# A state-space layer: B by transposes of one product, raw steps left in PSUM, and the next group's jobs dealt out anew

## The chip, the cores and the metric

The program runs on one core of a Trainium2 chip. The metric is device time in microseconds (us) of one execution, the median of several. Five engines work side by side, each through its own queue in order: TensorE (PE, products), VectorE (DVE), ScalarE (ACT), GpSimd (POOL) and SyncE (SP, which issues transfers). They meet only at semaphores.

## The reference

Six layers follow each other over 64 sequences of 128 steps and 128 features, each behind a residual sum and a normalisation. The change touches only the first, a selective state-space layer (the other five are left out here):

```python
def _ssm_forward(u, W_in, b_in, W_x, b_x, W_dt, b_dt, A_log, D, W_out, b_out):
    u_inner = u @ W_in.T + b_in
    x, z = jnp.split(u_inner, 2, axis=-1)              # 256 channels each
    dbc = x @ W_x.T + b_x
    delta_raw = dbc[..., :DT_RANK]                     # 8
    B_ssm = dbc[..., DT_RANK:DT_RANK + D_STATE]        # 16
    C_ssm = dbc[..., DT_RANK + D_STATE:]               # 16
    delta = jax.nn.softplus(delta_raw @ W_dt.T + b_dt)
    A = -jnp.exp(A_log)

    def step(h, xs):
        dt_t, x_t, Bt, Ct = xs
        dA = jnp.exp(dt_t[..., None] * A)
        dB = dt_t[..., None] * Bt[:, None, :]
        h = h * dA + x_t[..., None] * dB
        y_t = jnp.einsum('bdn,bn->bd', h, Ct)
        return (h, y_t)
    ...
    y = y + x * D
    y = y * (z * jax.nn.sigmoid(z))
    return y @ W_out.T + b_out

x = _layernorm(x + _L0_attn_ref(x, ...), axis=-1)
```

## The kernel before

`ssm_phase` works on 16 groups of four sequences (`GT` = 512 columns). A group is eight units, which I call steps 0 to 7: step p takes four of the 16 states (nq = p // 2) of one half of the 256 channels (half = p % 2). All arithmetic is fp32. In each step the engines do this:

- TensorE writes x·delta·B of the unit to the PSUM tile `db`: 16 small products (L349) of `dxT` with `diag`, a block-diagonal form of B. `db` has one buffer, so they wait for the scan of the step before (`h_ready`).
- ScalarE writes the decays `dA` of the next step: four Exp (L438).
- VectorE scans 2048 elements (L494), h = h·dA + db, and multiplies one state in four by C (L500, here hC on VectorE).
- GpSimd multiplies the other three by C (L556). Both factors lie in SBUF, on both engines.
- TensorE adds up y of two steps earlier: four products with the identity (L363). In the first unit of each half, x·D comes ahead of them as the product L358 ("the skip").

Beside these steps of group g, `head(g + 1, ..., p)` makes the inputs of the next group, a piece behind each step, and the code with `there(g - 1)` finishes the group before. Both stand in each engine's queue in the order of `step`, between two steps, and an engine that waits in one holds up the next step. The pieces of the next group:

- step 0: x (L306), read by ScalarE into `xi`. Step 1: w_x times x (L309, L310) gives C (rows 0 to 15) and the raw step (rows 32 to 39), read by ScalarE into `dbc` (L400). B is made apart, turned already: eight products with x as the stationary side (L314), to which VectorE adds the bias (L476, tile `Bt`).
- step 2: w_dt times the raw step (L322); ScalarE adds the bias and stores `dtr` (L407). Step 3: |dtr|, Exp, Ln (L410 to L414) into `spl`. Step 4: VectorE's `delta` = max(dtr, 0) + spl, 1024 elements (L481).
- steps 3 and 4: GpSimd makes `diag` (L536, four in all). Step 5: z (L328, Silu on ScalarE, L420) and, on GpSimd, dx = delta·x (L544). Step 6: eight transposes of dx (L334), copied to `dxT`.

Of the group before: VectorE's gate `yg` in steps 1 and 2 (L507); in step 4 the output product (L372) and, on VectorE, the residual sum r (L514) and its statistics (L117, L121); in step 3 GpSimd's `xr` = X + bias (L562), in step 5 its inverse deviation and shift (L126, L128, L571, L574); in step 6 ScalarE's normalised result (L452).

The PSUM is full: `db` has four banks, y two, `pj[0]` and `pj[1]` one each. All products for the next group and the output product share the last two.

## Time and profile before

| | us |
|---|---|
| median of 3 runs | 4159.24 |
| lowest and highest | 4155.75, 4160.47 |
| the profiled execution | 4173.35 |
| its span in the trace | 4171.5 |
| first scan of the layer starts | 33.56 |
| last scan of the layer starts | 981.67 |
| groups 1 to 14, mean each | 60.64 |

The layer takes the first 1004 us of the span; the other five phases, whose code is the same in both kernels, take the rest. A group is eight scans, so the start of one scan to the start of the next is the yardstick: the eight distances of a group add up to the group. The last row of the table is 848.90 us by 14. The page gives TensorE 83% busy over the span, VectorE 60%, GpSimd 48%, ScalarE 47%.

### The profile page before, as it was taken

Reading aid. Unit: us, or ns where it says so; the run is one execution under the profiler, and the core shown is the slowest. Engines: PE = TensorE matmul, PEld = TensorE weight load, DVE = VectorE, ACT = ScalarE, POOL = GpSimd, SP = SyncE. Lnnn points to the kernel's source line nnn. Section 1 sums busy time; section 2 is a strip of 40 time slices with the busy share of each in tenths; the row PEclk is TensorE's granted clock in tenths of the full one; section 3 lists DMA queues with packets and bytes.
Section 4 is the critical chain, followed back from the end, with each engine's and each line's share of the span. In section 5 each row is a group of like instructions: output and inputs, shape, how many; then the busy total and the mean of one; then the engine's idle time right before and its main releaser. Section 6 shows DMA issues by size and latency. Waiting matters only on the chain. (4 is left out here: it accounts for less than half of the span.)

```text
span 4171.5 us, 104540 instructions
## 1 busy us (share of the span) xinstructions
PE 3456.3 (83%) x41696; PEld 2257.9 (54%) x41696; DVE 2515.9 (60%) x5780; ACT 1949.0 (47%) x3810; POOL 2008.4 (48%) x1742
## 2 busy tenths in 40 slices
PE   7898889886888888777999979778888688888576
PEld 3444444443455555554666657645555455556476
DVE  6877877785656565474555548656666543433265
ACT  5555555552444444333555544245555344443154
POOL 5666766664567676561111116346666300102455
PEclk8999999997999999897999989879999788885598
DMA  3211212114600000000000000000000000000286
GB/s 117 77 74 76 76 68 77 70 74 156 218 2 2 2 2 2 15 15 4 5 5 5 4 10 1 10 1 0 0 0 0 10 5 6 5 4 14 76 260 194
DMA packets 48939, 181.24 MB, mean 43 GB/s; under 512 B 11678, under 2 KB 23073, under 8 KB 39360
## 3 DMA queue, kind: packets, MB, share of 16 engines
q1 hardware_dynamic: 44224, 167.68, 12.0%
q0 software_dynamic: 4352, 8.47, 0.6%
q8 instruction: 259, 4.24, 0.4%
q14 instruction: 104, 0.85, 0.1%
HBM read 167.13 MB, written 43.65 MB: 51 GB/s over the span
## 5 line engine op out<-in xcount | busy, mean ns | idle before, releaser
L494 DVE TENSOR_TENSOR_SCAN XC<-ssm_dA,ssm_db 128x2048 f32<-128x2048 f32 x128 | 565.6, 4419 | 148.3 <-PE ssm_db L349 124.7
L556 POOL TENSOR_TENSOR XC<-XC,XB 128x1536 f32<-128x1536 f32 x128 | 493.5, 3856 | 297.9 <-DVE XC L494 165.9
L363 PE MATMUL ssm_y<-XC,ssm_wt 128*128 128x512 f32 x1024 | 495.5, 629 | 1.6 <-POOL XC L556 1.6
L438 ACT ACTIVATE ssm_dA<-ssm_delta,ssm_nega 128x508 f32<-128x508 f32 x512 | 325.0, 707 | 107.3 <-DVE XC L494 107.3
L1138 POOL TENSOR_TENSOR self_pm<-self_pT,self_wt 128x512 f32<-128x512 f32 x256 | 320.9, 1291 | 68.7 <-ACT self_pT L912 68.7
L363 PEld LDWEIGHTS ssm_y<-XC,ssm_wt 128*128 128x128 f32 x1024 | 197.0, 200 | 230.8 <-issue 221.5
L2326 POOL TENSOR_TENSOR XC<-XC,gla_wt 128x512 f32<-128x512 f32 x128 | 160.7, 1276 | 159.5 <-ACT XC L2177 159.5
L1149 POOL TENSOR_TENSOR XC<-XC,XB 128x128 f32<-128x128 f32 x128 | 58.9, 460 | 363.9 <-DVE XB L1055 363.9
L349 PE MATMUL ssm_db<-XB,ssm_dxT 32*128 32x128 f32 x4096 | 175.4, 300 | 69.5 <-DVE XC L494 67.8
L126 POOL TENSOR_SCALAR narrow_rstd<-narrow_mv 128x4 f32<-128x4 f32 x16 | 3.6, 228 | 458.6 <-DVE narrow_mv L121 458.6
L349 PEld LDWEIGHTS ssm_db<-XB,ssm_dxT 32*128 32x128 f32 x4096 | 146.3, 199 | 135.0 <-DVE XC L494 110.9
L912 ACT ACTIVATE self_pT<-self_scores 128x512 f32<-128x512 f32 x256 | 132.2, 603 | 179.9 <-PE self_scores L799 179.9
L1404 ACT ACTIVATE narrow_pT<-narrow_scores 77x512 f32<-77x512 f32 x256 | 130.7, 592 | 132.4 <-PE narrow_scores L1337 132.4
L912 ACT ACTIVATE cross_pT<-cross_scores 77x512 f32<-77x512 f32 x256 | 130.8, 590 | 122.9 <-PE cross_scores L799 122.9
L2336 POOL TENSOR_TENSOR XC<-XC,gla_wt 128x512 f32<-128x512 f32 x128 | 160.9, 1278 | 35.0 <-ACT XC L2186 34.5
L1044 DVE TENSOR_TENSOR self_oT<-self_out,self_rinv 128x512 f32<-128x512 f32 x64 | 44.3, 692 | 207.2 <-ACT self_rinv L940 207.2
L1600 PEld LDWEIGHTS mlp_yp<-mlp_wt,mlp_h 128*128 128x128 f32 x1024 | 133.2, 192 | 58.1 <-issue 56.4
L1033 DVE TENSOR_REDUCE self_nmax<-self_scores 128x4 f32<-128x512 f32 x256 | 158.7, 683 | 9.2 <-PE self_scores L787 8.9
L1455 DVE TENSOR_TENSOR narrow_oT<-narrow_out,narrow_rinv 128x128 f32<-128x128 f32 x64 | 18.7, 292 | 239.1 <-ACT narrow_rinv L1413 173.3
L1044 DVE TENSOR_TENSOR cross_oT<-cross_out,cross_rinv 128x512 f32<-128x512 f32 x64 | 44.1, 688 | 186.7 <-ACT cross_rinv L940 178.5
L2259 DVE TENSOR_TENSOR XC<-gla_scores,gla_wt 128x512 f32<-128x512 f32 x128 | 82.4, 685 | 102.1 <-PE gla_scores L2051 102.1
L1628 ACT ACTIVATE mlp_h<-mlp_hp,mlp_bias 128x512 f32<-128x512 f32 x128 | 87.9, 687 | 108.6 <-PE mlp_hp L1592 108.4
(431 smaller groups left out, 8934.0 us busy)
## 6 DMA issues: line engine op xcount, KB each, us to landing
XB<-c_rows SPq DMA_DIRECT2D x64, 1024.0 KB, 4.5
experts_we<-in_w_experts SPq DMA_DIRECT2D x72, 579.0 KB
sorted<-in_padding SPq DMA_DIRECT2D x1, 33280.0 KB
experts_rt<-sorted SPq DMA_DIRECT2D x72, 65.0 KB
ssm_xT<-in_xT SPq DMA_DIRECT2D x16, 256.0 KB, 4.6
self_wt<-in_w_self SPq DMA_DIRECT2D x1, 1412.0 KB, 6.1
...
```

Source lines behind the costliest of these rows:

```text
L349: mm = pe.matmul(of_batch(db, b)[:, :, 32 * c:32 * c + 32], dxT[rows, slot, half, c, :], diag(slot, c)[rows, nq, :].rearrange("p (k t) -> ...
L363: mm = pe.matmul(yp[half][:, :].rearrange("p (b t) -> p b t", b=GROUP), ident, of_state(states(32, at), k), start=False, stop=(nq == 3 and ...
L438: o = act.activation(dA[:, p % 2, :].rearrange("p (b k t) -> p b k t", b=GROUP, k=4)[:, :, k, 1:T], by_batch(delta[:, slot, half, :])[:, : ...
L494: dve.tensor_tensor_scan(states(0, p).rearrange("p m t -> p (m t)"), dA[:, p % 2, :], db[:, :], 0.0, ALU.mult, ALU.add).then_inc(h_ready, 1)
L556: pool.tensor_tensor(states(32, p).rearrange("p (b k) t -> p b k t", k=4)[:, :, 0:3, :], states(0, p).rearrange("p (b k) t -> p b k t", k= ...
L912: act.activation(pT[0:TK, b % 2, r, :], sc[r][0:TK, :], ACT.Exp).then_inc(exp_ready, 1)
L1033: dve.tensor_reduce(nmax[:, r, :], sc[r][:, 0:4 * TK].rearrange("p (h t) -> p h t", h=4), AX.X, ALU.max, negate=True).then_inc(max_ready, 1)
L1138: pool.tensor_tensor(pm[:, b % 2, r, :].rearrange("p (h t) -> p h t", h=4), pT[:, b % 2, r, :].rearrange("p (h t) -> p h t", h=4), bcast(V ...
L1404: act.activation(pT[0:TK, b % 2, r, :], sc[r][0:TK, :], ACT.Exp).then_inc(exp_ready, 1)
L1600: mm = pe.matmul(yp[g % 2][:, b * C:(b + 1) * C], h[:, g % 2, j, b * T:(b + 1) * T], w3[:, j * C:(j + 1) * C], start=(j == 0), stop=(j == 3))
L2326: pool.tensor_tensor(a1(b, r), a1(b, r), bcast(tri, 1, 4), ALU.mult).then_inc(m1_pool, 1)
L2336: pool.tensor_tensor(a2(b, r), a2(b, r), bcast(tri0, 1, 4), ALU.mult).then_inc(m2_pool, 1)
```

## The change

B. w_x gets 80 rows: C in 0 to 15, the raw step in 32 to 39, B in 64 to 79, and a row 40 of zeros whose bias is 1.0. ScalarE reads rows 0 to 40 as before (batches reordered) and rows 64 to 79 in a second instruction, with their biases. Four transposes of those 16 rows, in step 2, replace the eight products of step 1, and ScalarE copies the result to `Bt` in VectorE's place.

Raw steps. Row 40 of `dbc` is a row of ones, and w_dt gets b_dt as its ninth row, so the product carries its bias. `dtr` is gone: |raw| is read from PSUM by two ScalarE instructions of 512 in step 2, and VectorE's `delta`, now in step 3, reads the raw steps from PSUM too (`pair`, the two banks as one tile). Until then both banks are held: the output product waits for `dt_ready`, and so does z, whose first half now goes to `pj[1]` and the second to `pj[0]`.

Jobs. The sum r moves from step 4 to 5, its statistics to 6; GpSimd's `xr` from 3 to 2, its inverse deviation from 5 to 6; the normalised result from 6 to 7. The skip of half 0 moves from the half's first unit (step 2) to its third (step 6). The second half of z, into `pj[0]`, waits for r (`r_ready`), which has been read from that bank.

```diff
-    PJ, N_ACT, DT, YS = 10, 9, 4, 2
+    PJ, N_ACT, DT, YS = 10, 9, 5, 2
...
+    SKIP = ((0, 2), (1, 0))
...
+        STEP = slice(32, 41)
+        INPUT = slice(64, 80)
...
-        pj = [ph.bank(f"pj{i}") for i in range(2)]
+        pair = ph.stack.enter_context(nc.psum_tensor(f"{name}_pj", [P, 2, GT], F32))
+        pj = [pair[:, i, :] for i in range(2)]
...
+                if p == 2:
+                    pe.wait_ge(proj_read, at + 4)
+                    pe.sem_inc(mark, 1)
                     for c in range(4):
-                        for j in range(2):
-                            mm = pe.matmul(pj[1][:, c * N:(c + 1) * N], xi[:, slot, j, c * P:(c + 1) * P],
-                                           w_xB[:, j * N:(j + 1) * N], start=(j == 0), stop=(j == 1))
+                        mm = pe.transpose(pj[1][:, c * N:(c + 1) * N], dbc[INPUT, c * P:(c + 1) * P], ident[INPUT, INPUT])
                     mm.then_inc(proj_mm, 1)
-                if p == 2:
-                    pe.wait_ge(proj_read, at + 3)
                     for j in range(2):
                         if j == 1:
-                            pe.wait_ge(Bt_ready, g + 1)
-                        pe.matmul(pj[j][:, :], w_dt[32:32 + 8, j * P:(j + 1) * P], dbc[32:32 + 8, :]).then_inc(proj_mm, 1)
+                            pe.wait_ge(proj_read, at + 5)
+                        pe.matmul(pj[j][:, :], w_dt[STEP, j * P:(j + 1) * P], dbc[STEP, :]).then_inc(proj_mm, 1)
                 if p == 5:
+                    pe.wait_ge(dt_ready, (g + 1) * DT)
                     for j in range(2):
-                        pe.wait_ge(proj_read, at + 4 + j)
-                        if j == 0 and needed(g - 1):
+                        if j == 1 and needed(g - 1):
                             pe.wait_ge(r_ready, g - 1)
-                        pe.matmul(pj[j][:, :], w_in[:, (2 + j) * P:(3 + j) * P], xT[:, slot, :]).then_inc(proj_mm, 1)
+                        pe.matmul(pj[1 - j][:, :], w_in[:, (2 + j) * P:(3 + j) * P], xT[:, slot, :]).then_inc(proj_mm, 1)
...
-                        if nq == 0:
-                            if needed(gy * YS):
-                                pe.wait_ge(y_step, (gy - 1) * YS + half + 1)
+                        if nq == 0 and needed(gy * YS):
+                            pe.wait_ge(y_step, (gy - 1) * YS + half + 1)
+                        if (half, nq) in SKIP:
                             pe.matmul(chunked(yp[half][:, :]), skip[:, half, :],
-                                      by_chunk(xi[:, slot if p >= 2 else 1 - slot, half, :]), start=True, stop=False)
+                                      by_chunk(xi[:, slot if p >= 2 else 1 - slot, half, :]), start=(nq == 0), stop=False)
...
                         if more(g) and there(g):
-                            pe.wait_ge(proj_read, (g + 1) * N_ACT + 4)
+                            pe.wait_ge(dt_ready, (g + 2) * DT)
...
                 if p == 2:
+                    act.wait_ge(proj_mm, at + 4)
...
+                    act.activation(Bt[:, :], pj[1][:, 0:GROUP * N], ACT.Identity).then_inc(proj_read, 1)
                     for j in range(2):
                         act.wait_ge(proj_mm, at + 5 + j)
...
-                        act.activation(dtr[:, j, :], pj[j][:, :], ACT.Identity, bias=b_dt[:, j:j + 1]).then_inc(proj_read, 1)
+                        act.activation(spl[:, j, :], pj[j][:, :], ACT.Abs).then_inc(dt_ready, 1)
                 if p == 3:
-                    act.wait_ge(proj_read, g * N_ACT + 5)
-                    act.activation(spl[:, :, :], dtr[:, :, :], ACT.Abs).then_inc(dt_ready, 1)
...
-                if p == 4:
-                    dve.wait_ge(dt_ready, g * DT + 3)
+                if p == 3:
+                    dve.wait_ge(dt_ready, g * DT + 4)
...
                     dve.scalar_tensor_tensor(delta[:, slot].rearrange("p a t -> p (a t)"),
-                                             dtr[:, :, :].rearrange("p a t -> p (a t)"), 0.0,
+                                             pair[:, :, :].rearrange("p a t -> p (a t)"), 0.0,
                                              spl[:, :, :].rearrange("p a t -> p (a t)"), ALU.max, ALU.add)\
```

What this makes of the queues, at three places of a group in the loop. L349 and L350 are the products into `db`, L363 and L364 those of y (one line on in the kernel after).

TensorE from the end of step 1's pieces to the w_dt products of step 2; L314 and L318 make B, L322 and L323 the raw steps, L358 is the skip. Before:

```order
L314 MATMUL ssm_pj<-ssm_wt,ssm_xi 128x16 x8
L345 REGISTER_ALU
L349 MATMUL ssm_db<-XB,ssm_dxT 128x4x32 [waits ssm_h_ready]
L349 MATMUL ssm_db<-XB,ssm_dxT 128x4x32 x15
L357 ISA
L358 MATMUL ssm_y<-ssm_xi,ssm_skip 128x512 [waits ssm_y_step]
L363 MATMUL ssm_y<-XC,ssm_wt 128x512 [waits ssm_hC_pool,ssm_hC_dve]
L363 MATMUL ssm_y<-XC,ssm_wt 128x512 x3
L318 REGISTER_ALU
L322 MATMUL ssm_pj<-ssm_dbc,ssm_wt 128x512 [waits ssm_proj_read]
L321 REGISTER_ALU
L322 MATMUL ssm_pj<-ssm_dbc,ssm_wt 128x512 [waits ssm_Bt_ready]
```

After:

```order
L346 REGISTER_ALU
L350 MATMUL ssm_db<-XB,ssm_dxT 128x4x32 [waits ssm_h_ready]
L350 MATMUL ssm_db<-XB,ssm_dxT 128x4x32 x15
L357 ISA
L364 MATMUL ssm_y<-XC,ssm_wt 128x512 [waits ssm_hC_pool,ssm_hC_dve,ssm_y_step]
L364 MATMUL ssm_y<-XC,ssm_wt 128x512 x3
L315 REGISTER_ALU
L318 MATMUL ssm_pj<-ssm_wt,ssm_dbc 128x16 [waits ssm_proj_read]
L318 MATMUL ssm_pj<-ssm_wt,ssm_dbc 128x16 x3
L323 MATMUL ssm_pj<-ssm_dbc,ssm_wt 128x512
L322 REGISTER_ALU
L323 MATMUL ssm_pj<-ssm_dbc,ssm_wt 128x512 [waits ssm_proj_read]
```

The 16 passes of L314 stood between w_x and the next step's products; now nothing does, the skip is gone from this step, and four transposes stand ahead of w_dt.

VectorE from one scan (L494, printed as SCALAR_TENSOR_TENSOR) to the next, with delta (L481), r (L514) and the statistics. Before, steps 4 to 5:

```order
L494 SCALAR_TENSOR_TENSOR XC<-ssm_dA,ssm_db 128x2048 [waits ssm_hC_pool,ssm_dA_ready,ssm_dB_mm]
L199 REGISTER_ALU [waits ssm_h_ready]
L500 TENSOR_TENSOR XC<-XC,XB 128x4x128 [waits ssm_y_mm,ssm_c_in0]
L514 TENSOR_TENSOR ssm_r<-ssm_pj,ssm_xr 128x512 [waits ssm_x_out,ssm_xr_ready,ssm_out_mm]
L117 BN_STATS ssm_stats<-ssm_r 128x6 [waits ssm_r_ready]
L117 BN_STATS ssm_stats<-ssm_r 128x6 x3
L121 BN_AGGR ssm_mv<-ssm_stats 128x2 [waits ssm_vec]
L121 BN_AGGR ssm_mv<-ssm_stats 128x2 x3
L478 REGISTER_ALU
L481 SCALAR_TENSOR_TENSOR ssm_delta<-ssm_dtr,ssm_spl 128x1024 [waits ssm_dA_ready,ssm_dt_ready]
L490 REGISTER_ALU
L494 SCALAR_TENSOR_TENSOR XC<-ssm_dA,ssm_db 128x2048 [waits ssm_hC_pool,ssm_dA_ready,ssm_dB_mm]
```

After, steps 3 to 5:

```order
L494 SCALAR_TENSOR_TENSOR XC<-ssm_dA,ssm_db 128x2048 [waits ssm_hC_pool,ssm_dA_ready,ssm_dB_mm]
L500 TENSOR_TENSOR XC<-XC,XB 128x4x128 [waits ssm_y_mm,ssm_c_in1,ssm_h_ready]
L478 ISA
L481 SCALAR_TENSOR_TENSOR ssm_delta<-ssm_pj,ssm_spl 128x1024 [waits ssm_dA_ready,ssm_dt_ready]
L490 REGISTER_ALU
L494 SCALAR_TENSOR_TENSOR XC<-ssm_dA,ssm_db 128x2048 [waits ssm_hC_pool,ssm_dA_ready,ssm_dB_mm]
L201 REGISTER_ALU [waits ssm_h_ready]
L500 TENSOR_TENSOR XC<-XC,XB 128x4x128 [waits ssm_y_mm,ssm_c_in0]
L490 REGISTER_ALU
L494 SCALAR_TENSOR_TENSOR XC<-ssm_dA,ssm_db 128x2048 [waits ssm_hC_pool,ssm_dA_ready,ssm_dB_mm]
L500 TENSOR_TENSOR XC<-XC,XB 128x4x128 [waits ssm_y_mm,ssm_c_in0,ssm_h_ready]
L514 TENSOR_TENSOR ssm_r<-ssm_pj,ssm_xr 128x512 [waits ssm_x_out,ssm_xr_ready,ssm_out_mm]
```

One distance held r, statistics and delta; now delta has step 3, r step 5, and the statistics have gone to step 6.

GpSimd from step 5's multiplication by C (L556, after: L557) on; dx is L544, after: L545. Before:

```order
L556 TENSOR_TENSOR XC<-XC,XB 128x4x384 [waits ssm_y_mm,ssm_c_in0,ssm_h_ready]
L126 TENSOR_SCALAR ssm_rstd<-ssm_mv 128x4 [waits ssm_vec,ssm_x_out]
L127 REGISTER_ALU
L128 TENSOR_TENSOR ssm_rstd<-ssm_rstd,ssm_power 128x4 [waits ssm_pool_step]
L570 REGISTER_ALU
L571 TENSOR_TENSOR ssm_shift<-ssm_mv,ssm_rstd 128x4 [waits ssm_pool_step]
L572 REGISTER_ALU
L574 TENSOR_SCALAR ssm_shift<-ssm_shift 128x4 [waits ssm_pool_step]
L540 REGISTER_ALU
L542 REGISTER_ALU [waits ssm_dt_ready]
L544 TENSOR_TENSOR ssm_dx<-ssm_delta,ssm_xi 128x4x4x32 [waits ssm_proj_mm]
L544 TENSOR_TENSOR ssm_dx<-ssm_delta,ssm_xi 128x4x4x32
```

After:

```order
L557 TENSOR_TENSOR XC<-XC,XB 128x4x384 [waits ssm_y_mm,ssm_c_in0,ssm_h_ready]
L541 ISA
L543 REGISTER_ALU [waits ssm_dt_ready]
L545 TENSOR_TENSOR ssm_dx<-ssm_delta,ssm_xi 128x4x4x32 [waits ssm_proj_mm]
L545 TENSOR_TENSOR ssm_dx<-ssm_delta,ssm_xi 128x4x4x32
L553 REGISTER_ALU
L557 TENSOR_TENSOR XC<-XC,XB 128x4x384 [waits ssm_y_mm,ssm_c_in1,ssm_h_ready]
L126 TENSOR_SCALAR ssm_rstd<-ssm_mv 128x4 [waits ssm_vec,ssm_x_out]
L127 REGISTER_ALU
L128 TENSOR_TENSOR ssm_rstd<-ssm_rstd,ssm_power 128x4 [waits ssm_pool_step]
L571 REGISTER_ALU
L572 TENSOR_TENSOR ssm_shift<-ssm_mv,ssm_rstd 128x4 [waits ssm_pool_step]
```

The inverse deviation and shift stood between step 5 and dx; now they follow step 6's multiplication.

## Rows read from the trace of the kernel before

**Rows 1.** The page: its head.
```profile
span 4171.5 us, 104540 instructions
```
**Rows 2.** Busy time by stretch, groups 1 to 14: us, busy (count) of each engine, PEclk.
```profile
89.90:149.80 59.90, 54.37 (x381) 29.24 (x381) 48.22 (x29) 32.90 (x51) 41.77 (x20) 0.94 0.21 76
...
sum 848.90, PE 755.77 PEld 406.54 DVE 674.84 ACT 460.15 POOL 583.85; mean PE 53.98 PEld 29.04 DVE 48.20 ACT 32.87 POOL 41.70
```
**Rows 3.** VectorE in order of time, group 8: start, us, operation, [idle before <-releaser].
```profile
514.01 4.42 DVE L494 TENSOR_TENSOR_SCAN XC<-ssm_dA,ssm_db 128x2048 f32<-128x2048 f32 x1 [0.74 <-PE ssm_db L349]
...
520.38 4.42 DVE L494 TENSOR_TENSOR_SCAN XC<-ssm_dA,ssm_db 128x2048 f32<-128x2048 f32 x1 [1.06 <-PE ssm_db L349]
...
528.85 4.42 DVE L494 TENSOR_TENSOR_SCAN XC<-ssm_dA,ssm_db 128x2048 f32<-128x2048 f32 x1 [0.81 <-POOL XC L556]
...
536.14 4.42 DVE L494 TENSOR_TENSOR_SCAN XC<-ssm_dA,ssm_db 128x2048 f32<-128x2048 f32 x1 [1.44 <-PE ssm_db L349]
...
541.86 4.42 DVE L494 TENSOR_TENSOR_SCAN XC<-ssm_dA,ssm_db 128x2048 f32<-128x2048 f32 x1 [0.47 <-PE ssm_db L349]
...
549.30 3.42 DVE L481 SCALAR_TENSOR_TENSOR ssm_delta<-ssm_dtr,ssm_spl 128x1024 f32<-128x1024 f32 x1
552.64 4.41 DVE L494 TENSOR_TENSOR_SCAN XC<-ssm_dA,ssm_db 128x2048 f32<-128x2048 f32 x1
...
558.34 4.42 DVE L494 TENSOR_TENSOR_SCAN XC<-ssm_dA,ssm_db 128x2048 f32<-128x2048 f32 x1 [0.57 <-PE ssm_db L349]
...
570.21 4.42 DVE L494 TENSOR_TENSOR_SCAN XC<-ssm_dA,ssm_db 128x2048 f32<-128x2048 f32 x1 [6.72 <-PE ssm_db L349]
```
**Rows 4.** TensorE in order of time, group 8, same columns.
```profile
519.14 1.17 PE L349 MATMUL ssm_db<-XB,ssm_dxT 32*128 32x128 f32 x32
...
525.72 1.96 PE L314 MATMUL ssm_pj<-ssm_wt,ssm_xi 128*128 128x16 f32 x16
527.61 1.17 PE L349 MATMUL ssm_db<-XB,ssm_dxT 32*128 32x128 f32 x32
528.71 1.12 PE L358 MATMUL ssm_y<-ssm_xi,ssm_skip 128*128 128x512 f32 x2
529.67 3.60 PE L363 MATMUL ssm_y<-XC,ssm_wt 128*128 128x512 f32 x8
533.20 0.69 PE L322 MATMUL ssm_pj<-ssm_dbc,ssm_wt 8*128 8x512 f32 x1
...
545.26 1.95 PE L372 MATMUL ssm_pj<-ssm_wt,ssm_yg 128*128 128x128 f32 x16
547.13 1.17 PE L349 MATMUL ssm_db<-XB,ssm_dxT 32*128 32x128 f32 x32
...
551.77 1.88 PE L328 MATMUL ssm_pj<-ssm_xT,ssm_wt 128*128 128x512 f32 x4
```
**Rows 5.** TensorE in order of time, group 8, around its step 6.
```profile
566.15 1.96 PE L334 MATMUL ssm_pj<-ssm_wt,ssm_dx 128*128 128x128 f32 x8 [4.25 <-POOL ssm_dx L544]
568.05 2.09 PE L349 MATMUL ssm_db<-XB,ssm_dxT 32*128 32x128 f32 x32
```
**Rows 6.** VectorE by line, whole run: ns min/median/max, first and last start.
```profile
L481 DVE SCALAR_TENSOR_TENSOR ssm_delta<-ssm_dtr,ssm_spl x16: 1226/3426/4459, 20.2 to 914.2; 128x1024 f32<-128x1024 f32 x16
...
L500 DVE TENSOR_TENSOR XC<-XC,XB x128: 691/693/1604, 38.0 to 986.1; 128x512 f32<-128x512 f32 x128
...
L507 DVE TENSOR_TENSOR ssm_yg<-ssm_y,ssm_zs x32: 682/684/692, 101.3 to 994.0; 128x512 f32<-128x512 f32 x32
```
**Rows 7.** GpSimd in order of time, group 8, step 5.
```profile
561.15 0.23 POOL L126 TENSOR_SCALAR ssm_rstd<-ssm_mv 128x4 f32<-128x4 f32 x1
...
563.55 2.47 POOL L544 TENSOR_TENSOR ssm_dx<-ssm_delta,ssm_xi 128x512 f32<-128x512 f32 x2
```
**Rows 8.** ScalarE in order of time, group 8, step 3.
```profile
540.40 1.06 ACT L414 ACTIVATE ssm_spl<-ssm_spl 128x1024 f32<-128x1024 f32 x1
```
**Rows 9.** TensorE by stretch: us, busy (count), PEclk, DMA share, GB/s.
```profile
265.00:270.00 5.00, 5.00 (x30) 0.63 0.00 0
```

More of the change, by code:

```diff
@@ L164, in ssm_phase @@
         zs = ph.sb("zs", [P, 2, 2, GT])
-        dbc = ph.sb("dbc", [64, GT])
+        dbc = ph.sb("dbc", [80, GT])
         Bt = ph.sb("Bt", [P, GROUP * N])
-        dtr = ph.sb("dtr", [P, 2, GT])
         spl = ph.sb("spl", [P, 2, GT])
@@ L363, in step @@
                             mm = pe.matmul(yp[half][:, :].rearrange("p (b t) -> p b t", b=GROUP), ident,
-                                           of_state(states(32, at), k), start=False, stop=(nq == 3 and k == 3))
+                                           of_state(states(32, at), k), start=(k == 0 and nq == 0 and (half, 0) not in SKIP),
+                                           stop=(nq == 3 and k == 3))
                         mm.then_inc(y_mm, 1)
@@ L419, in head @@
                             act.wait_ge(y_step, (g - 1) * YS)
-                        act.activation(zs[:, slot, j, :], pj[j][:, :], ACT.Silu, bias=b_in[:, 2 + j:3 + j]).then_inc(proj_read, 1)
+                        act.activation(zs[:, slot, j, :], pj[1 - j][:, :], ACT.Silu, bias=b_in[:, 2 + j:3 + j]).then_inc(proj_read, 1)
                     act.preload_act_table_set("natural_log_exp_and_others")
@@ L448, in step @@
                             decay(g + 1, 1 - slot, 0)
-                    if p == 6 and there(g - 1):
+                    if p == 7 and there(g - 1):
                         act.wait_ge(pool_step, g * 4)
@@ L508, in step @@
                             .then_inc(y_step, 1)
-                    if p == 4 and there(g - 1):
+                    if p == 5 and there(g - 1):
                         dve.wait_ge(out_mm, g)
@@ L514, in step @@
                         dve.tensor_tensor(r[:, :, :], by_batch(pj[0][:, :]), xr[:, :, :], ALU.add).then_inc(r_ready, 1)
+                    if p == 6 and there(g - 1):
                         dve.wait_ge(r_ready, g)
@@ L531, in head @@
                 if p in (3, 4):
-                    pool.wait_ge(Bt_ready, g + 1)
+                    pool.wait_ge(proj_read, g * N_ACT + 5)
                     if needed((g - 1) * U):
```

45 lines of the change are left out of this document (20 added, 25 removed).

## The prediction

> **What bounds the kernel now.** I read the busy times first, then one group of the loop engine by engine in order of time, and at each scan asked what it had waited for. The layer in question is the first 1004 us of a span of 4171.5 [rows 1]; the rest is the same code. Groups 1 to 14 take 848.90 / 14 = 60.64 us each, and TensorE is busy for 53.98 of them [rows 2]. So no engine is full, but TensorE is near: what is taken off another engine's chain can shorten a group by about six us and little more, unless TensorE's own work shrinks or it is busy now at a lower clock.
>
> The eight distances between scans of group 8 are 6.37, 8.47, 7.29, 5.72, 10.78, 5.70 and 11.87 us for steps 0 to 6 [rows 3], and a step 7 that carries no piece, which I take at 5.9. The floor is seen in step 5: scan 4.42, then the products into `db`, which must wait for it, and 1.24 from their start to the next scan (527.61 to 528.85) [rows 3, 4], 5.70 in all. Everything above it is a piece of some other group that stands in a queue. The scans of steps 1 and 2 wait for TensorE, the scan after step 4 for VectorE's own row of small work, and the one after step 6 idles for 6.72 us behind TensorE [rows 3], which itself waited 4.25 us for GpSimd's dx [rows 5].
>
> **Unit prices**, start to start at the full clock [rows 4]: products into `db` 1.10, skip 0.96, y 3.53, output product 1.87, both halves of z 1.88. The w_dt pair and the products behind it overlap: y ends at 533.20, scan 3 starts at 536.14 and so would a `db` product at 534.90, hence 1.70 for the pair. B's sixteen passes cost 1.89, 0.118 each.
>
> **The change, step by step.** Each sum is the new distance from this scan to the next.
>
> Step 0, untouched: 6.37.
>
> Step 1: L314 is gone, so the next `db` products start where it started: 525.72 - 519.14 = **6.58** [rows 4]. ScalarE's second read of `dbc`, and that VectorE no longer adds B's bias, lie beside this and cost nothing; the read is wanted only after y.
>
> Step 2: the skip leaves, four transposes come. They are single passes with 16 moving columns like those of L314, so 4 x 0.118 = 0.47; the bounds are nothing and 0.95 (half of the eight dx transposes, which took 1.90 at the low clock [rows 5]). 1.10 + 3.53 + 0.47 + 1.70 = **6.80**. The second w_dt product waits for ScalarE's copy of 64 columns; a pass over 1024 takes 1.06 [rows 8], so the copy is shorter than the 0.9 us of the first product, which covers it. Behind the wait stand step 3's `db` products; were the cover gone, up to 0.3.
>
> Step 3: now VectorE carries delta. Before, it took 3.42 us [rows 3]. The same instruction took 1226 ns at its fastest, in the first group, where GpSimd was not multiplying, and 3426 in the median; L500, with both inputs in SBUF, ranges from 691 to 1604, while L507, which has one input in PSUM, never leaves 682 to 692 [rows 6], although GpSimd is multiplying in the same time. Delta will have one input in PSUM, so I take 1.23. 4.42 + 0.69 + 1.23 with 0.06 of waits is **6.40**, 0.7 over the floor; TensorE's 1.10 + 0.96 + 3.53 = 5.59 is hidden by it. ScalarE must be ready: its Ln ended at 541.46, 5.3 us after scan 3 began [rows 3, 8]; one pass over 1024 columns leaves this stretch (the |raw| is taken in step 2, as dtr was), so 4.3, against 5.1 at which VectorE asks. Bounds 5.72 and 9.7 (below).
>
> The rule of the Trainium skill here is in "SBUF — State Buffer", section "Who interferes with whom": a VectorE instruction with two SBUF inputs contends with a GpSimd instruction that reads SBUF, the later one blocks for the whole of the other, and one SBUF input outside the two-port modes does not contend. The trace agrees with its first half: 1226 ns alone, 3426 in company. By the rule step 3 is 6.40, without it 9.65, a rival below.
>
> Step 4: VectorE has only hC. TensorE's `db` products begin at scan 3's end (4.46), then 1.10 + 3.53 + 1.87 (the output product, whose new wait for delta is met by then), then 1.24: 12.20 after scan 3, so 12.20 - 6.40 = **5.80** in place of 10.78. This is the largest single gain: r, statistics and a blocked delta lay end to end.
>
> Step 5: the one new wait on the path. The second half of z must wait for r, and r now stands behind scan 5 and hC. Scan and start of hC 4.46, a GpSimd `diag` instruction that may still hold hC up 0.3 (bounds 0 and 0.9, the spread of L500 [rows 6]), hC 0.6, r 0.69, wait 0.1, half of z 0.94, 1.24: **8.33** in place of 5.70. Queued behind it on TensorE are step 6's `db` products, so VectorE pays all of it; ScalarE's Silu and table loads follow, but the decays of step 7 have over 3 us to spare. If r cost nothing here it would be 1.10 + 3.53 + 1.88 = 6.51.
>
> Step 6: the inverse deviation and shift, 561.15 to 563.55 [rows 7], no longer stand before dx. GpSimd's product of step 5 was done 8.5 us after scan 5 started (552.64 to 561.15) [rows 3, 7]; with the 0.3 of above that is 8.8, and dx, 2.47 long, ends at 11.3, which is 3.0 after scan 6 starts. TensorE asks for it after 1.10 + 0.96 (the skip, moved here) + 3.53, that is 4.35 after scan 6 starts, so the wait of 4.25 us is gone with 1.3 to spare. The transposes took 1.90 at the low clock [rows 5], so 0.95: **6.54**. VectorE's statistics (about 1.4 us behind hC) just fit. What is late next is GpSimd's inverse deviation after step 6's product, done about 10.8 us after scan 6; ScalarE's result in step 7 needs it, and nobody needs that for the next 6 us.
>
> Step 7: 5.9.
>
> **The sum.** 6.37 + 6.58 + 6.80 + 6.40 + 5.80 + 8.33 + 6.54 + 5.9 = 52.7 us, against 60.64: 7.9 per group, of which 1.4 is TensorE work that is no longer done and most of the rest waiting. The 60.64 holds a price of the clock too: in 265 to 270 us TensorE had a granted clock of 0.63 [rows 9], right behind its wait for dx; that is a mix of the 2.4 and 1.2 GHz levels. In the new order its longest idle time is some 1.8 us, in step 5 (8.33 - 6.51), and I count the loop at the full clock. 14 x 7.9 = 111. The first group has no predecessor to finish and the last no successor to prepare; I give both together 5 us (bounds 0 and 12). The start-up waits on GpSimd's `diag` and dx, which do not change. So 116 us off the profiled execution's 4173.35 (4057), and off the median, which is 14 us or 0.3% lower, 4159.24 - 116 = **4043**.
>
> **The rivals.**
>
> Delta stays blocked. If VectorE waits for GpSimd with a PSUM input as well, or the two-bank read is slow, delta starts when GpSimd's product ends, some 8.5 us after scan 3 as in step 5 now [rows 3, 7], and step 3 is 9.7. That is 3.3 a group, 49 us: 4092. For it: the same instruction, the same neighbour. Against it: L507's narrow spread. 0.09. This is also the case in which a part of the change doesn't do what it says.
>
> The low clock comes back. TensorE still idles a little in steps 3, 5 and 7. The worst group of before shows what it costs there: step 6 took 11.87 in group 8. Up to 2 us a group, 10 to 30 us: about 4065. 0.12.
>
> The wait for r is hidden. If VectorE gets to r earlier than I think, or TensorE's y is what is late, step 5 is 6.5: 4017. 0.06.
>
> Slower: TensorE bound at the low clock. The new loop leaves TensorE idle for 0.8 us in step 3, 1.8 in step 5 and a little in step 7, so it is some 94% busy (its 53.98 us of now hold passes at the low clock), and a lower clock is no longer absorbed. At the low level `db` takes 2.09 in place of 1.10 [rows 5] and y double its 3.53, some 4.3 us more per step. With about two such steps in each group the gain is gone; with three it is 75 us over before, 4234. In the rows the low clock followed waits of TensorE, which get fewer, so 0.04, and 0.01 that it comes out just even.
>
> **How the numbers follow.** The forecast has 0.68, with its own range 4030 to 4060 from the bounds of the transposes, of step 5 and of the end groups. The range takes in that, the clock rival and half of the early r: 4020 to 4080, which leaves out the blocked delta and the slow case. A measurement of this kernel can tell about 0.2% (8 us) from no change. Faster: 0.68 + 0.09 + 0.12 + 0.06 = 0.95; within 0.2%: 0.01; slower: 0.04.
>
> **What the profile after would show.** Delta at 1.2 us, 16 times, with a small spread; if its median is above 3 the first rival holds. The scans' distances in the order 6.4, 6.6, 6.8, 6.4, 5.8, 8.3, 6.5, 5.9; in step 5 TensorE's second z product behind r, idle for more than a us. No wait for dx ahead of the transposes. A granted clock of 1.0 through the groups, and TensorE busy for more than nine tenths. A last scan at about 870 us. If step 5 is short and step 6 long, I have put a wait in the wrong place; if all steps are longer by a little, the unit prices were read too low.

## The result and the profile after

The changed kernel took 4013.55 us (median of 4 runs, 4011.05 to 4014.82) against 4159.85 for the kernel before: a ratio of 0.9651, interval 0.9632 to 0.9670, 146 us less. The 4159.85 is the median of the three runs shown above and a fourth, slow one of 5071.11 that the ratio leaves out (4159.24 without it). The forecast was 4043 with a range of 4020 to 4080. The direction was right; the time lies 29.5 us under the forecast and 6.5 us under the range.

The profiled execution took 4014.37 us. Its page, the head, the busy times and the granted clock (compare [rows 1]):

```profile
span 4012.5 us, 104116 instructions
## 1 busy us (share of the span) xinstructions
PE 3369.8 (84%) x41504; PEld 2200.6 (55%) x41504; DVE 2465.1 (61%) x5764; ACT 1948.3 (49%) x3826; POOL 1997.8 (50%) x1742
...
PEclk8999999988999999979999989889999788887598
```

The view by stretch, groups 1 to 14, answers to [rows 2]; the columns are the same:

```profile
84.15:136.19 52.04, 49.49 (x369) 26.02 (x369) 44.94 (x29) 31.36 (x49) 41.10 (x20) 1.00 0.24 88
136.19:188.19 52.00, 49.53 (x369) 26.03 (x369) 44.93 (x29) 32.67 (x52) 40.97 (x20) 1.00 0.25 87
...
760.58:812.57 51.99, 49.43 (x369) 25.96 (x369) 44.93 (x28) 32.67 (x52) 40.98 (x20) 1.00 0.22 81
sum 728.42, PE 693.11 PEld 364.34 DVE 628.95 ACT 456.95 POOL 574.73; mean PE 49.51 PEld 26.02 DVE 44.93 ACT 32.64 POOL 41.05
```

A group takes 728.42 / 14 = 52.03 us where it took 60.64. TensorE's granted clock stands at 1.00 in all fourteen, and it is busy for 49.5 of the 52.0 us, 95%. VectorE's busy time has fallen from 48.2 to 44.9 us a group, of which delta makes 2.2 (3.42 to 1.22) and the bias that it no longer adds another 0.2 (L476, 225 ns in the trace of before).

VectorE in order of time, group 8, from the scan of step 0 to that of the next group's (compare [rows 3]; L500 is hC, L514 is r, L117 and L121 the statistics):

```profile
448.38 4.42 DVE L494 TENSOR_TENSOR_SCAN XC<-ssm_dA,ssm_db 128x2048 f32<-128x2048 f32 x1 [0.74 <-PE ssm_db L350]
...
461.21 4.42 DVE L494 TENSOR_TENSOR_SCAN XC<-ssm_dA,ssm_db 128x2048 f32<-128x2048 f32 x1 [0.70 <-PE ssm_db L350]
...
467.66 4.42 DVE L494 TENSOR_TENSOR_SCAN XC<-ssm_dA,ssm_db 128x2048 f32<-128x2048 f32 x1 [0.70 <-PE ssm_db L350]
472.21 0.69 DVE L500 TENSOR_TENSOR XC<-XC,XB 128x512 f32<-128x512 f32 x1
472.82 1.22 DVE L481 SCALAR_TENSOR_TENSOR ssm_delta<-ssm_pj,ssm_spl 128x1024 f32<-128x1024 f32 x1
473.95 4.41 DVE L494 TENSOR_TENSOR_SCAN XC<-ssm_dA,ssm_db 128x2048 f32<-128x2048 f32 x1
...
479.89 4.42 DVE L494 TENSOR_TENSOR_SCAN XC<-ssm_dA,ssm_db 128x2048 f32<-128x2048 f32 x1 [0.64 <-PE ssm_db L350]
484.34 0.81 DVE L500 TENSOR_TENSOR XC<-XC,XB 128x512 f32<-128x512 f32 x1
485.07 0.68 DVE L514 TENSOR_TENSOR ssm_r<-ssm_pj,ssm_xr 128x512 f32<-128x512 f32 x1
488.10 4.42 DVE L494 TENSOR_TENSOR_SCAN XC<-ssm_dA,ssm_db 128x2048 f32<-128x2048 f32 x1 [2.35 <-PE ssm_db L350]
492.66 0.69 DVE L500 TENSOR_TENSOR XC<-XC,XB 128x512 f32<-128x512 f32 x1
493.27 0.87 DVE L117 BATCH_NORM_STATS2 ssm_stats<-ssm_r 128x6 f32<-128x128 f32 x4
494.29 0.38 DVE L121 BATCH_NORM_AGGREGATE ssm_mv<-ssm_stats 128x2 f32<-128x6 f32 x4 [0.16 <-DVE ssm_stats L117]
494.59 4.41 DVE L494 TENSOR_TENSOR_SCAN XC<-ssm_dA,ssm_db 128x2048 f32<-128x2048 f32 x1
```

Five of the eight scans now wait for the products into `db` by 0.64 to 1.06 us, two wait for nothing, and the one long idle time left is the 2.35 us ahead of step 6's scan. TensorE's side of the same group (compare [rows 4, 5]):

```profile
464.70 0.23 PE L318 MATMUL ssm_pj<-ssm_wt,ssm_dbc 16*128 16x16 f32 x1
464.71 0.69 PE L323 MATMUL ssm_pj<-ssm_dbc,ssm_wt 9*128 9x512 f32 x1
464.79 0.33 PE L318 MATMUL ssm_pj<-ssm_wt,ssm_dbc 16*128 16x16 f32 x3
465.25 1.02 PE L323 MATMUL ssm_pj<-ssm_dbc,ssm_wt 9*128 9x512 f32 x2
465.68 0.59 PE L350 MATMUL ssm_db<-XB,ssm_dxT 32*128 32x128 f32 x7
...
485.81 1.12 PE L329 MATMUL ssm_pj<-ssm_xT,ssm_wt 128*128 128x512 f32 x2 [1.49 <-DVE ssm_r L514]
486.86 1.17 PE L350 MATMUL ssm_db<-XB,ssm_dxT 32*128 32x128 f32 x32
...
492.36 1.04 PE L335 MATMUL ssm_pj<-ssm_wt,ssm_dx 128*128 128x128 f32 x8
```

The second half of z waits 1.49 us for r, which is the new wait; the transposes of dx at 492.36 wait for nobody, where they stood behind 4.25 us. By the profile the first w_dt product (L323) starts 0.01 us after the first transpose of B (L318), so that the other three lie within it, and the next step's `db` products begin while the second is still running.

The distances between scans, from the starts of L494 (medians over groups 1 to 14, of the two middle values the higher one, us; "forecast" is the list in the prediction):

```
step          0     1     2     3     4     5     6     7    group
before      6.37  8.46  7.30  5.72 10.79  6.23 10.10  5.89   60.64
forecast    6.37  6.58  6.80  6.40  5.80  8.33  6.54  5.90   52.7
after       6.37  6.45  6.45  6.30  5.94  8.21  6.49  5.87   52.03
```

No group of after is off its group time by more than 0.05 us, while before step 5 lay between 5.70 and 6.62 and step 6 between 8.80 and 11.87. The first group went from 56.33 to 50.75 us and the last from 42.85 to 41.69; the scans run from 33.40 to 854.26 where they ran from 33.56 to 981.67, that is 127.3 us less. Of the 159 us between the two profiled executions this leaves some 32 that the loop cannot hold.

### The profile page after: what moved, and what is told of

Read it like the earlier page. It is cut to its first block and busy times, and to the rows that moved or that the text cites. A ratio compares the mean times of both kernels' runs of the same rounds, so it can differ in the third digit from the quotient of the medians.

```text
span 4012.5 us, 104116 instructions
## 1 busy us (share of the span) xinstructions
PE 3369.8 (84%) x41504; PEld 2200.6 (55%) x41504; DVE 2465.1 (61%) x5764; ACT 1948.3 (49%) x3826; POOL 1997.8 (50%) x1742
## 5 line engine op out<-in xcount | busy, mean ns | idle before, releaser
L494 DVE TENSOR_TENSOR_SCAN XC<-ssm_dA,ssm_db 128x2048 f32<-128x2048 f32 x128 | 565.5, 4418 | 109.0 <-PE ssm_db L350 96.1
L557 POOL TENSOR_TENSOR XC<-XC,XB 128x1536 f32<-128x1536 f32 x128 | 505.5, 3949 | 180.5 <-DVE XC L494 127.7
L364 PE MATMUL ssm_y<-XC,ssm_wt 128*128 128x512 f32 x1024 | 472.8, 605 | 2.5 <-POOL XC L557 2.3
L364 PEld LDWEIGHTS ssm_y<-XC,ssm_wt 128*128 128x128 f32 x1024 | 187.8, 191 | 216.0 <-issue 204.6
L350 PEld LDWEIGHTS ssm_db<-XB,ssm_dxT 32*128 32x128 f32 x4096 | 134.7, 187 | 99.3 <-DVE XC L494 65.0
L350 PE MATMUL ssm_db<-XB,ssm_dxT 32*128 32x128 f32 x4096 | 160.4, 285 | 24.8 <-DVE XC L494 23.2
```

The costliest lines, as they stand in the source:

```text
L350: mm = pe.matmul(of_batch(db, b)[:, :, 32 * c:32 * c + 32], dxT[rows, slot, half, c, :], diag(slot, c)[rows, nq, :].rearrange("p (k t) -> ...
L364: mm = pe.matmul(yp[half][:, :].rearrange("p (b t) -> p b t", b=GROUP), ident, of_state(states(32, at), k), start=(k == 0 and nq == 0 and ...
L494: dve.tensor_tensor_scan(states(0, p).rearrange("p m t -> p (m t)"), dA[:, p % 2, :], db[:, :], 0.0, ALU.mult, ALU.add).then_inc(h_ready, 1)
L557: pool.tensor_tensor(states(32, p).rearrange("p (b k) t -> p b k t", k=4)[:, :, 0:3, :], states(0, p).rearrange("p (b k) t -> p b k t", k= ...
```

## The experiments

**1. The same two kernels again, in a new series of runs.** The kernels are unchanged. A series is a set of runs timed side by side; the three new series each ran on a chip of its own.

> The kernel before, unchanged, profiled once more. The measured gain was 146 us where the layer's own scans account for 127 (first scan to last: 948.1 us before, 820.9 after); the other phases, whose code is the same, took 3167 us before and 3134 after in the two profiles. Theory A (chance of one execution: TensorE's clock and the timing of instruction loading differ each time): here the other phases differ from 3167 by some 10 us, and single phases by up to 20, in either direction. Theory B (the other phases run faster because of where the layer leaves them, in the program or in time): the other phases repeat within 15 us of 3167 and each phase within a few us, and the difference to the kernel after stays. The layer itself repeats within 3 us (1004) under both.

> The changed kernel, unchanged, profiled once more. The layer repeats at 878 us within 2 (its groups 52.0 each). Theory A: the other phases scatter around 3134 by 10 us or more and overlap with those of the kernel before. Theory B: they repeat, near 3134, and the ratio to the kernel before stays at 0.965, which is 20 us more than the layer gives.

Measured: before 4140.62 us (10 runs) against 4140.0 for the same kernel timed beside it, ratio 1.0011 (0.9984 to 1.0039); after 4017.82 (4 runs), ratio 0.9693 (0.9643 to 0.9743), 122 us less. The layer's phase, start to start from the profiles, took 1003.7 us in before and 878.8 in after; in the first pair it was 1004.1 and 878.3. So the layer gives 125 us both times, and the kernel before is what moved, by 20 us, while after stayed within 4. The rest of the program differs like this (us by phase, in the program's order; the five layers behind the first stand in eight phases; "rest" is all but the layer; "after third" is from experiment 8):

```
              layer   self    mlp  cross    mlp   mix    gla narrow experts    rest
before       1004.1  709.5  157.4  596.6  144.7  96.1  576.2  536.1   350.8  3167.4
before again 1003.7  706.4  157.4  597.9  145.3  94.9  578.8  528.5   324.6  3133.8
after         878.3  717.9  156.8  594.8  144.9  94.4  585.7  517.3   322.4  3134.2
after again   878.8  717.8  156.7  591.1  145.3  94.4  585.7  525.5   325.5  3142.1
after third   876.9  713.1  157.2  591.0  145.4  94.6  582.8  514.7   325.8  3124.5
```

The rest of before repeated 33.6 us shorter, and 26.2 of these are in experts. Without experts the rest is 2816.6 and 2809.2 in before and 2811.8, 2816.6 and 2798.7 in after. Of the 159 us between the two first profiles the layer makes 125.8, experts 28.4 and all else 4.8. The long experts phase differs from the short one at its start. The view by stretch from its first transfer to the first one of the experts' weights (from and to, us, PE busy and count, PEclk, DMA share, GB/s), in the profile of before:

```profile
3820.72:3931.34 110.62, 75.85 (x354) 0.50 0.12 40
```

and in that of after:

```profile
3690.11:3773.93 83.82, 74.29 (x354) 0.50 0.15 48
```

The same work took 27 us longer in the first profile of before, and the view of waits names for it only a releaser outside the core's own engines (waiting engine, buffer and line, then the releaser with us, times and the longest):

```profile
DVE experts_best L2591 <- remote: 28.0, 4, 9.1
ACT XB L2547 <- remote: 12.0, 2, 9.5
DVE experts_key L2608 <- remote: 7.7, 2, 5.6
```

The profile of after has no such line, and neither has that of before again: its stretch took 83.9 us. The stretch took 84 us in the profiles of all kernels of two series of runs and 107 in those of the third (experiments 4 to 7), whichever kernel it was, and lines with "remote" stand there in all four profiles of the third and in none of the others. So it does not belong to the change. What "remote" stands for there was not found.

**2. r one step earlier.** From after:

```diff
-                    if p == 5 and there(g - 1):
+                    if p == 4 and there(g - 1):
                         dve.wait_ge(out_mm, g)
```

> The sum r goes back from step 5 to step 4 on VectorE, all else as in the changed kernel. Theory: in step 5 TensorE waits for r (1.49 us, after which z's second half and the next db products follow), and r in step 4 costs nothing, since the output product is done just when hC of step 4 ends. Expected: step 5 from 8.21 to about 6.5 us, step 4 from 5.94 to 6.0 at most, groups of 50.4 in place of 52.0, in all 23 us less than the changed kernel (3990). Rival: r in step 4 delays scan 5 by its own 0.69, so 13 us less. Rival: step 5 stays at 8.2 because ScalarE or GpSimd holds it there.

Measured distances: 6.37 6.45 6.45 6.30 5.94 **6.45** **6.96** 5.88, group 50.75; layer 860.7 us; 3992.33 us in all, ratio 0.9633 (0.9584 to 0.9682). VectorE in step 4, and TensorE in step 6, both of group 9:

```profile
521.18 0.68 DVE L514 TENSOR_TENSOR ssm_r<-ssm_pj,ssm_xr 128x512 f32<-128x512 f32 x1
521.91 4.42 DVE L494 TENSOR_TENSOR_SCAN XC<-ssm_dA,ssm_db 128x2048 f32<-128x2048 f32 x1
```
```profile
533.05 1.09 PE L335 MATMUL ssm_pj<-ssm_wt,ssm_dx 128*128 128x128 f32 x8 [0.28 <-POOL ssm_dx L545]
534.07 1.17 PE L350 MATMUL ssm_db<-XB,ssm_dxT 32*128 32x128 f32 x32
```

The wait for r is gone and costs step 4 nothing: r fills the 0.64 us in which VectorE idled before that scan. So the 1.76 us of step 5 (8.21 - 6.45) are the price of r's place behind scan 5, as the prediction had it (8.33 - 6.51 = 1.82). Of these 0.47 come back in step 6, which was not expected: GpSimd makes dx behind its product of step 5, which waits for scan 5 as before, and TensorE now asks for dx 0.28 us before it is done. So the layer is 18 us shorter than in after again (878.8), where 14 x 1.6 = 23 had been expected; the medians differ by 25.

**3. The statistics too.** The same edit, and

```diff
-                    if p == 6 and there(g - 1):
+                    if p == 5 and there(g - 1):
                         dve.wait_ge(r_ready, g)
```

> As the kernel with r in step 4, and the statistics of r move from step 6 to 5. Theory: in step 6 VectorE and TensorE end together (6.49 by both), so taking 1.3 us off VectorE there gives nothing more than the wait for a semaphore: step 6 6.45 to 6.49; in step 5, where TensorE's y and z take 6.5, VectorE has 4.42 + 0.7 + 1.4 = 6.5, also a tie. Groups within 0.1 us of the kernel with r in step 4. Rival: VectorE was what held step 6, and step 6 falls to 6.3 or less.

Measured: step 5 6.49, step 6 6.92, group 50.76; layer 858.5. Where the statistics stand makes no difference between these two. The whole took 4003.23 us (0.9671, 0.9621 to 0.9720), 11 more than the kernel of experiment 2 with a layer 2 us shorter: this is the size of what the other phases do by themselves.

**4. dx earlier as well.** Experiment 2's edit, and on GpSimd

```diff
-                if p in (3, 4):
+                if p in (3, 5):
...
-                if p == 5:
+                if p == 4:
                     pool.wait_ge(dt_ready, (g + 1) * DT)
```

which puts dx into step 4 and the second half of `diag` into step 5.

> As the kernel with r in step 4, and GpSimd makes dx in step 4 and the second half of diag in step 5, swapped. With r in step 4, step 6 grew from 6.49 to 6.96: there the transposes wait for dx, which GpSimd makes behind its product of step 5. Theory: dx made a step earlier is never waited for, and step 6 is TensorE's 1.10 + 0.96 + 3.43 + 0.97, some 6.5 us. Groups of 50.3 in place of 50.75, 7 us less in all. Rival: the second half of diag, or GpSimd's product of step 5, is then late, and a later step grows by as much; or VectorE's statistics hold step 6 at 6.49 to 6.9 anyhow.

Measured: step 5 6.45, step 6 6.49, group 50.28, layer 850.8 us, 4013.13 us against 4175.92 for before in the same series, ratio 0.9626 (0.9591 to 0.9661). GpSimd in steps 4 and 5, and TensorE in step 6, group 9:

```profile
517.48 2.49 POOL L545 TENSOR_TENSOR ssm_dx<-ssm_delta,ssm_xi 128x512 f32<-128x512 f32 x2
519.93 3.88 POOL L557 TENSOR_TENSOR XC<-XC,XB 128x1536 f32<-128x1536 f32 x1
```
```profile
525.56 1.04 PE L335 MATMUL ssm_pj<-ssm_wt,ssm_dx 128*128 128x128 f32 x8
```

dx is done by 519.97, 5.6 us before TensorE turns it, and TensorE's last wait in step 6 is gone.

**5. Delta with two inputs in SBUF again.** A tile `none` of zeros takes the place of the PSUM pair, so delta leaves the raw step out; its time is read as that of an instruction of the same shape.

```diff
-                                             pair[:, :, :].rearrange("p a t -> p (a t)"), 0.0,
+                                             none[:, :, :].rearrange("p a t -> p (a t)"), 0.0,
```

> The changed kernel, but delta in step 3 takes its first input from a tile of zeros in SBUF in place of the raw steps in PSUM; so the raw step is left out of the maximum, and nothing else differs, in order or in waits. Theory (the PSUM input is what frees VectorE from GpSimd): delta waits until GpSimd's product of step 3 has ended, some 8.5 us after the scan started, and step 3 is 9.6 us in place of 6.30; groups near 55 us. Rival (delta was slow before because of where it stood, behind r and the statistics): delta takes 1.2 us as now, and step 3 stays at 6.3.

Measured: step 3 9.55 us in place of 6.30, step 4 5.70 or 6.62, step 5 8.10 to 9.57, step 6 6.47 to 7.71, groups 55.2 to 57.3; layer 941.8; 4130.23 us (one run). GpSimd and VectorE in step 3, group 8:

```profile
505.51 3.95 POOL L559 TENSOR_TENSOR XC<-XC,XB 128x1536 f32<-128x1536 f32 x1 [1.35 <-PE ssm_y L365]
```
```profile
506.08 4.47 DVE L483 SCALAR_TENSOR_TENSOR ssm_delta<-ssm_none,ssm_spl 128x1024 f32<-128x1024 f32 x1
510.47 4.41 DVE L496 TENSOR_TENSOR_SCAN XC<-ssm_dA,ssm_db 128x2048 f32<-128x2048 f32 x1
```

GpSimd's product runs to 509.46; delta starts at 506.08, within it, and ends 1.1 us after it, about its own length alone. In after the same instruction takes 1218 ns beside the same product:

```profile
L481 DVE SCALAR_TENSOR_TENSOR ssm_delta<-ssm_pj,ssm_spl x16: 1217/1218/1225, 19.3 to 785.0; 128x1024 f32<-128x1024 f32 x16
```

Both halves of what the Trainium skill says in "SBUF — State Buffer", section "Who interferes with whom", are borne out: two SBUF inputs block behind a GpSimd instruction that reads SBUF, one does not. Of the first rival (step 3 at 9.7, a group 3.3 longer) the size was right and the condition false. The PSUM input is worth 3.25 us in step 3. In the three groups whose granted clock stayed at 1.00 in every step (7, 8 and 10) that is all, 55.2 to 55.3 us; in the other eleven it fell to between 0.77 and 0.94 in two of steps 4 to 6, and they took 55.8 to 57.3.

**6. Twelve transposes more.** B is turned four times over.

```diff
-                    for c in range(4):
+                    for c in (0, 1, 2, 3) * 4:
```

> The changed kernel with the four transposes of B done four times over, to the same place. In the changed kernel step 2 took 6.45 where 6.80 was forecast, with 0.47 for four transposes. Theory (they run beside the w_dt products, which use other rows of the array, and cost nearly nothing): twelve more add well under their 1.4 us, and single w_dt products start among them. Rival (they cost 0.118 each and another term was too high): step 2 grows by 1.4 us, to 7.9.

Measured: step 2 took 7.20 or 7.21 us in seven of the fourteen groups, 0.76 over after's 6.45, so 0.06 for each of the twelve, and up to 8.10 in the others; step 3 took 6.30 in three groups (1, 8 and 10) and 7.35 to 8.72 in the other eleven, where the granted clock over step 3 was 0.73 to 0.86. Groups took about 52.8 (three), 54.4 to 54.5 (ten) and 56.13; layer 909.9; 4061.01 us (one run). Four stretches of group 7 (PEclk is the third from last):

```profile
421.00:426.00 5.00, 5.00 (x42) 2.55 (x41) 4.26 (x4) 3.83 (x6) 3.95 (x1) 1.00 0.00 0
426.00:431.00 5.00, 5.00 (x56) 3.13 (x55) 3.50 (x4) 2.44 (x6) 3.33 (x1) 0.97 0.51 210
431.00:436.00 5.00, 5.00 (x10) 1.98 (x8) 3.80 (x1) 4.65 (x7) 1.85 (x2) 0.69 0.00 0
436.00:441.00 5.00, 5.00 (x42) 2.61 (x41) 4.37 (x3) 1.38 (x3) 4.33 (x2) 1.00 0.00 0
```

and TensorE there, in steps 2 and 3:

```profile
426.66 0.98 PE L318 MATMUL ssm_pj<-ssm_wt,ssm_dbc 16*128 16x16 f32 x13
427.43 0.69 PE L323 MATMUL ssm_pj<-ssm_dbc,ssm_wt 9*128 9x512 f32 x1
427.49 0.33 PE L318 MATMUL ssm_pj<-ssm_wt,ssm_dbc 16*128 16x16 f32 x3
...
431.73 4.77 PE L364 MATMUL ssm_y<-XC,ssm_wt 128*128 128x512 f32 x8
```

Thirteen transposes now stand ahead of the first w_dt product and take 0.83 us, 0.064 each, and the last three lie beside it as they do in after. So the 0.06 is what such a transpose takes when nothing runs beside it, about half of L314's 0.118.

The granted clock fell to 0.69, a mix of the 2.4 and 1.2 GHz levels, without an idle time just before it: TensorE was busy for the whole 20 us. Its last wait (0.93 us, up to 409.02) lay some 21 us back, and after has the same wait (1.01 in group 8) at 1.00 throughout. What stood ahead of the fall, and does not stand in after, was the row of small products; the same row stood in the three groups that kept the full clock, so it does not always bring the fall. y (L364) took 4.77 in place of 3.60 for it.

**7. Only the inverse deviation moved, in the kernel before.** GpSimd's piece goes from step 5 to step 6, ScalarE's result from 6 to 7.

```diff
-                    if p == 6 and there(g - 1):
+                    if p == 7 and there(g - 1):
                         act.wait_ge(pool_step, g * 4)
...
-                    if p == 5 and there(g - 1):
+                    if p == 6 and there(g - 1):
                         pool.wait_ge(vec, g * VEC)
```

> One part alone, on the kernel before: GpSimd's inverse deviation and shift go from step 5 to step 6, and ScalarE's normalised result from 6 to 7. Theory: dx comes 2.4 us earlier, so TensorE's wait for it in step 6 falls from 4.25 to about 1.8, and step 6 from a median of 10.1 to about 7.7; with only one long wait left (3.44 us in step 4) TensorE's clock stays high in more of the groups. Groups of some 57.5 to 58 in place of 60.6. Rival: the low clock comes from the wait in step 4 alone, and steps 5 and 6 keep a scatter of a us or more from group to group.

Measured: step 6 7.3 to 7.6 us in place of 8.80 to 11.87, step 5 5.70 or 6.62 where it lay between them, steps 0 to 4 as in before, groups 57.7 to 58.6, layer 964.3; 4128.12 us (one run) against 4175.92. TensorE in one group:

```profile
478.64 1.17 PE L349 MATMUL ssm_db<-XB,ssm_dxT 32*128 32x128 f32 x32 [3.46 <-DVE XC L494]
479.75 3.70 PE L363 MATMUL ssm_y<-XC,ssm_wt 128*128 128x512 f32 x8
485.18 1.09 PE L334 MATMUL ssm_pj<-ssm_wt,ssm_dx 128*128 128x128 f32 x8 [1.74 <-POOL ssm_dx L544]
```

The move alone brings 2.6 us a group, 40 of the layer's 125. The wait for dx falls from 4.25 to 1.74, and the transposes run in 1.09 in place of 1.96, at the full clock. That 1.74 us are left here and none in after fits with TensorE's coming later there: it waits 1.49 us for r in step 5 and has 0.96 of skip in step 6. The 3.46 us wait in front is for scan 5, which is late because r, statistics and delta stand ahead of it.

**8. After and the two moves of experiment 4, side by side.** The kernels are those of experiments 1 and 4.

> The changed kernel once more, timed against the kernel before on one chip, to see how much of the 146 us belongs to the change. In ten profiles so far the stretch of the experts phase up to its first weight transfer took either 83.9 us (five) or 107 to 111 us (five), whatever the kernel, and all four of one call alike; the first profile of the kernel before had the long form, the first of the kernel after the short one. Theory: the long form belongs to the chip or its state and not to the kernel, so the two kernels share it here, and the difference of the medians is what the layer gives, 122 to 128 us, ratio 0.970. Rival: the short form comes with the changed kernel, and the difference is again 146 or more, ratio 0.965.

> The kernel with r and dx both in step 4, timed beside the changed kernel. Its layer took 850.8 us where the changed kernel's took 878.8. Expected: 28 us less than the changed kernel in the medians, 0.993 of it, 150 to 155 less than the kernel before. Rival: part of it is given back in later phases through TensorE's clock, which scatters there by 10 us.

Measured: after 4013.81 us (5 runs), ratio 0.9690 (0.9670 to 0.9710), 134 under the 4147.61 of before in the same series; with r and dx in step 4, 3988.23 (3973.63 to 3999.97), ratio 0.9608 (0.9588 to 0.9629). The layer took 876.9 and 851.2 us, and the two medians differ by the same 26 (28 had been expected). The 134 lie between what was expected if only the layer counts (122 to 128) and the 146 of the first pair. The version with both moves beats both kernels.

**9. The skip of half 0 back in step 2.** From after:

```diff
-    SKIP = ((0, 2), (1, 0))
+    SKIP = ((0, 0), (1, 0))
```

> The changed kernel, but the skip of half 0 is back in its first unit, in step 2. Theory: step 2 is TensorE's, so it grows by the whole 0.96, from 6.45 to 7.4; step 6 does not shrink, since VectorE's scan, hC and statistics end together with TensorE there (6.49). Groups of 53.0 in place of 52.0. Rival: step 6 was TensorE's alone and falls by 0.9, so the group stays at 52.0 and the move was worth nothing.

Measured: step 2 7.31 (+0.86), step 6 6.38 (-0.11), groups 52.78, one of 55.02; layer 891.1; 4021.28 us (one run). VectorE around step 6 of one group:

```profile
493.97 4.42 DVE L494 TENSOR_TENSOR_SCAN XC<-ssm_dA,ssm_db 128x2048 f32<-128x2048 f32 x1 [2.35 <-PE ssm_db L350]
498.42 0.69 DVE L500 TENSOR_TENSOR XC<-XC,XB 128x512 f32<-128x512 f32 x1
```

The skip costs nearly its length in step 2 and almost nothing in step 6, where VectorE's row is what is late: in after the scan at 494.59 has no idle time before it. The 0.11 are in that row too. hC waits for y of two steps earlier (`y_mm`), and there y stands behind the skip: hC starts 4.56 us after its scan's start in after (488.10 to 492.66) and 4.45 here. By the rows of after, y ends at 492.53, and GpSimd's product, which waits for the same y, starts at 492.70 behind 1.79 us of idle time put down to it. The remaining row of scan, hC and statistics makes the 6.38.

## Why the predicted time was too high

**The steps.** Each of the eight distances came out within 0.15 us of the forecast except that of step 2. The sum of 52.7 is thus right in its order and its waits:

- Step 0: 6.37, as said.
- Step 1: 6.45 for 6.58. With L314 gone the products into `db` follow w_x's, as the prediction read it. The 0.13 lie ahead of L314's place: from y to the first w_x product 3.63 us in before and 3.54 in after, between the two w_x products 0.88 and 0.85. Why is not shown.
- Step 2: 6.45 for 6.80, the largest miss. The term 4 x 0.118 = 0.47 was the one mis-sized: it measured nothing, the prediction's own lower bound. In the rows of after w_dt starts 0.01 us behind the first transpose. Two things make it so: a transpose of 16 rows takes 0.064 where nothing runs beside it, not 0.118, and the last three run beside w_dt (experiment 6). Against that, w_dt's row starts 3.63 us behind y's and not 3.53.
- Step 3: 6.30 for 6.40. Delta takes 1218 ns in all sixteen cases, as forecast; the first rival fell, and experiment 5 shows what it would have been.
- Step 4: 5.94 for 5.80. What is late is TensorE, as said; counted from scan 3 it is 12.23 for 12.20, so most of the excess is what step 3 took less.
- Step 5: 8.21 for 8.33. The only new wait is where the prediction put it, 1.49 us at TensorE for r; experiment 2 takes it away and with it 1.76 us. The third rival (r hidden) fell; hC was held up by 0.12 (0.81 for 0.69).
- Step 6: 6.49 for 6.54, for another reason than given. The sum came from TensorE's chain with 0.96 for the skip. VectorE's row of statistics, which the prediction said would "just fit", is the bound, and the skip adds 0.11 by holding up hC (experiment 9). That the two sums agree is luck. The removed piece was put right: experiment 7 shows it alone.
- Step 7: 5.87 for 5.9.

Together 52.03 for 52.7, that is 8.6 us a group for 7.9: 14 x 0.7 = 10 us more. The first and the last group gave 5.6 + 1.2 = 6.8 us for 5. So the loop gave 127 us where the sum said 116, and the last scan starts at 854 and not at about 870.

**The clock.** The forecast that the loop runs at the full clock held in all fourteen groups, and the second rival and the slower one fell. Their reason is open to doubt, though: they tied a low clock to idle time. In after TensorE idles for 1.49 us in step 5 and keeps 1.00, and in experiment 6 it falls to 0.69 on a TensorE that has been busy for some 21 us. In before the 0.63 [rows 9] did follow a wait; that it takes a wait is not so. The slower rival's price is also off by its own terms: three low steps at 4.3 us in 14 groups add 181 us to 4043, which is 4224 and not 4234.

**The rest of the program.** Had the sum said 127, it would have given 4032, inside the range; the measured 4013.55 is 18 us lower still. The step that failed is the last line of the sum, 4159.24 - 116: the 116 was 11 short (the term of the transposes, 0.47 in 14 groups, is 6.6 of it), and it was taken off the median of the runs shown as if all outside the loop stayed equal, which left another 18 us out of the forecast.

In three series after took 4013.55, 4017.82 and 4013.81, and before 4159.85, 4140.0 and 4147.61 beside it (4175.92 in a fourth, in which after itself was not run). The differences are 146, 122 and 134; the layer's was 126 and 125 in the two pairs of profiles. So an excess of 20 us over the layer's gain was there in the first pair only; in the others it was about none and some 8.

In the first pair's profiles experts accounts for 28.4 us and narrow for 18.8 in after's favour, self and gla for 17.9 against it. Experts' share follows the series of runs and not the kernel. For narrow the table shows 11 us between profiles of after, and 8 between those of before. Self and gla go with the layer ahead of them: in the eight profiles in which it took 891 us or less they took 713 to 719 and 580 to 586, in four of the five with a longer layer 706 to 710 and 576 to 579, and with experiment 5's 713.7 and 580.0. Narrow goes rather the other way, so that the three together show no difference (1822 and 1814 in before, 1821, 1829 and 1811 in after).

The low end of the range lay 23 us under the forecast, with nothing in it for a scatter of this size; the profiled execution, 14 us over its median, was the sign of it.

What remains open: what the waits on "remote" are; whether the runs of before in the first pair that have no profile were of that long kind too (their profile was; their 4159 lies between the 4140 of a short series and the 4176 of the long one); and why self and gla are longer behind a shorter layer. That the long kind made the 18 us is likely by the profiles, and not shown for the medians.
